# Cross attention in a two-layer decoder: token-major keys, one mixing group, query weights split one stage earlier, another order of the transposes

## The chip, the cores and the metric

The kernel runs on one core of a Trainium2 chip, in one launch. The metric is device time in microseconds (us) of one execution, as the median of some executions. The core has a matrix engine (TensorE, PE in the profile; its weight loads are PEld), VectorE (DVE), ScalarE (ACT), GpSimd (POOL) and the queue that starts transfers (SyncE, SP). Matmul results go to PSUM, eight banks of 128 x 512 float32; GpSimd works on SBUF alone.

## The reference

A decoder of two layers on 32 sequences of 64 tokens with 256 features, so 2048 rows. Each layer has three sublayers, `x = x + f(norm(x))`. The change touches two of the second layer: the state-space sublayer (only as the place where weights of the next one are prepared) and the cross attention behind it:

```python
q = rms(xn @ Wq + bq)  # 16 heads of 128; RMSNorm over each head, eps 1e-6
k = rms(ctx @ Wk + bk)  # 4 heads of 128
v = ctx @ Wv + bv
probs = softmax(q @ k.T / sqrt(128) + mask)  # each k/v head serves 4 query heads; 64 x 64 in each sequence
x = x + (probs @ v) @ Wo
```

`ctx` is the second input, 64 rows for each sequence. All of it is float32; the kernel's big products use pairs (below).

## The kernel before

The sublayers run one after another, with a barrier of all engines between them: `differential_attention`, `feature_attention`, `selected_update`, `state_space`, `grouped_attention` (the cross attention) and `mixture`.

The cross attention works in 16 tiles of 128 rows (two sequences each). One turn t of `pipeline` works at three tiles at once: it finishes tile t-1 (mixing and output product), does scores and softmax of tile t, and projects and norms the queries and keys of tile t+1; rows of tile t+2 are normed and transposed. Turns -2 to 0 fill the pipeline, turns 1 to 13 are a hardware loop, turns 14 to 16 drain it. Nothing is scheduled by a planner: each engine's order is the order of the code in its `turn`, and semaphores (`wait_ge`) hold an engine until another has got so far. So an instruction that waits holds all that stand behind it on its engine.

A precise float32 product is made as three passes (`three_passes`): the operands are split into a high part (float32r) and a low part (the rest), and high x high, low x high and high x low are added in PSUM. The high parts are copied by ScalarE or VectorE, the low parts are a subtraction on VectorE or GpSimd.

What a turn does, by name:
- `query(n, g)`: one of four quarters (512 columns) of the query projection, 6 matmuls of 512 columns, alternating between PSUM banks 0 and 1; VectorE adds the bias (`biased`, writes `q`), ScalarE squares (`square`, writes `q_scaled`), VectorE sums by head (`query_sums`, in two halves of 8 heads), ScalarE makes the inverse root by Ln and Exp (`query_rms`, writes `q_inv`), GpSimd multiplies (`scale_queries`, writes `q_scaled`), TensorE transposes (`turn_queries`, four quarters), ScalarE copies to `qT` (`take_queries`).
- Keys: `w_k` times `ctxT_k`, made feature-major in 16 matmul records of plain float32 of 128 columns (bank 2); ScalarE adds the bias and squares; the squares are split in two and summed over partitions by two matmuls with a matrix of ones (`k_sums`); ScalarE takes Ln and Exp of 128x512; VectorE multiplies to `kT`.
- Values: three passes of `ctxT_high`/`ctxT_low` with `w_v` (bank 3), which stand between the second and third quarter of `turn_queries`.
- Scores: `kT` and `qT` give scores with the keys on partitions, banks 4 and 5; ScalarE copies them (`scoresT`), TensorE transposes them to banks 6 and 7, VectorE adds the mask, takes the maximum, subtracts it; ScalarE takes Exp; VectorE sums, inverts (`inv`) and multiplies (`probs`). TensorE transposes `probs` to banks 4 and 5, ScalarE and VectorE make `probsT_high` and `probsT_low`.
- `mix(n, pair)`: values times probabilities, two of four key heads per pair; both pairs use banks 4 and 5, so the second waits until ScalarE (`take_mixed`) and VectorE (`mixed_low`) have read the first. Then the output product, 48 matmuls of 256 columns, into bank 6.

The query weights (2 MB) are loaded in the state-space stage to `staged`, and split at the start of the cross attention: VectorE and ScalarE copy the high halves, VectorE and GpSimd subtract.

## Time and profile before

| | us |
|---|---|
| median of 3 runs (1475.48 to 1477.69) | 1475.66 |
| the profiled execution's own time | 1476.98 |
| its span, first to last instruction | 1475.1 |

| engine | busy, share of the span |
|---|---|
| PE | 87% |
| DVE | 68% |
| ACT | 50% |
| POOL | 27% |

The cross attention runs from about 749 to 1170 us of the span, and its state-space predecessor from about 612 to 749 us. A turn in the middle of the cross attention takes 23.96 us. The share of the whole span says little on one stage; the stage is read from its own windows and from the timeline of one turn.

### The profile page before, as it was taken

The page shows a single profiled execution, that of the slowest core. Times are in us where ns is not written, and L with a number is a line of the kernel's source. Part 1 is how long each engine was busy: PE and PEld are TensorE (multiplying, and loading weights), DVE is VectorE, ACT ScalarE, POOL GpSimd, SP SyncE. Part 2 cuts the span into 40 slices and gives each one's busy share as a digit, 9 for nine tenths or more (in the row PEclk, how much of TensorE's full clock was granted, in tenths as well). Part 3 has the DMA queues.
Part 4 walks back from the last instruction along what each step waited for, and adds up shares of the span by engine and source line. Part 5 has one row for each costly group of instructions (what it writes and reads, how often), then busy time and mean ns, then how long its engine had stood idle before and what let it go on. Part 6 is the DMA issues. An engine that isn't in the chain of part 4 may idle for free. (4 is left out here: it accounts for less than half of the span.)

```text
span 1475.1 us, 28417 instructions
## 1 busy us (share of the span) xinstructions
PE 1290.2 (87%) x10124; PEld 1045.9 (71%) x10124; DVE 997.2 (68%) x1870; ACT 740.9 (50%) x1504; POOL 399.8 (27%) x488
## 2 busy tenths in 40 slices
PE   4888987199999984799958999999998599999998
PEld 3666665045555654478946878788887599999998
DVE  4767676267777745579855777777786557655555
ACT  1555555157777773430025667666666345333332
POOL 1112120344444410148625313132222021112210
PEclk9999999579999997579978999999999799999999
DMA  3000000345444400200030000000000110010001
GB/s 107 1 0 0 0 0 1 77 115 133 109 126 126 110 22 7 95 1 0 0 126 8 11 11 11 10 14 11 11 11 8 44 44 22 22 38 29 2 1 58
DMA packets 53385, 56.15 MB, mean 38 GB/s; under 512 B 7779, under 2 KB 49347, under 8 KB 50627
## 3 DMA queue, kind: packets, MB, share of 16 engines
q1 hardware_dynamic: 53318, 55.25, 13.5%
q8 instruction: 43, 0.70, 0.2%
q14 instruction: 24, 0.20, 0.0%
HBM read 44.35 MB, written 10.49 MB: 37 GB/s over the span
## 5 line engine op out<-in xcount | busy, mean ns | idle before, releaser
L677 DVE TENSOR_REDUCE fa_neg_max<-psum 128x2 f32<-128x512 f32 x256 | 167.7, 688 | 58.3 <-PE psum L854 57.6
L738 ACT ACTIVATE fa_probs<-psum 128x1024 f32<-128x1024 f32 x128 | 130.2, 1018 | 39.9 <-PE psum L865 36.2
L1607 PE MATMUL psum<-mo_xT_high,mo_w_high 128*128 128x256 f32 x512 | 145.6, 284 | 3.6 <-DVE mo_w_low L2278 3.6
L1607 PE MATMUL psum<-mo_xT_low,mo_w_high 128*128 128x256 f32 x512 | 145.2, 284 | 0.0
L1607 PE MATMUL psum<-mo_xT_high,mo_w_low 128*128 128x256 f32 x512 | 144.6, 282 | 0.0
L854 PE MATMUL psum<-fa_k_stack,fa_q_stack 72*128 72x256 bf16 x512 | 104.0, 288 | 35.6 <-DMA fa_k_stack<-k_parts 34.3
L2233 ACT ACTIVATE mo_silu<-psum 128x256 f32<-128x256 f32 x128 | 49.1, 384 | 159.9 <-PE psum L1607 159.8
L2367 DVE TENSOR_TENSOR mo_mid<-mo_silu,psum 128x256 f32<-128x256 f32 x128 | 53.7, 419 | 96.6 <-ACT mo_silu L2233 96.5
L1728 POOL TENSOR_TENSOR ga_q_scaled<-ga_q,ga_q_inv 128x1024 f32<-128x1024 f32 x32 | 62.1, 1941 | 165.9 <-ACT ga_q_inv L1769 165.9
L1607 PEld LDWEIGHTS psum<-mo_xT_high,mo_w_high 128*128 128x128 f32 x512 | 97.4, 190 | 4.0 <-DVE mo_w_low L2278 4.0
L1607 PEld LDWEIGHTS psum<-mo_xT_low,mo_w_high 128*128 128x128 f32 x512 | 97.5, 190 | 0.0
L1607 PEld LDWEIGHTS psum<-mo_xT_high,mo_w_low 128*128 128x128 f32 x512 | 97.4, 190 | 0.0
L854 PEld LDWEIGHTS psum<-fa_k_stack,fa_q_stack 72*128 72x128 bf16 x512 | 41.2, 100 | 77.2 <-DVE fa_neg_max L677 33.6
L865 PE MATMUL psum<-fa_q_stack,fa_k_stack 75*128 75x256 bf16 x512 | 79.2, 278 | 7.7 <-DMA fa_q_stack<-fa_max_rows 7.7
L258 POOL TENSOR_TENSOR da_keys<-da_rot,da_head_mask 128x1024 f32<-128x1024 f32 x16 | 30.4, 1897 | 186.7 <-DVE da_rot L386 186.7
L2179 POOL TENSOR_TENSOR mo_w_low<-mo_raw,mo_w_high 128x512 fp32r<-128x512 f32 x21 | 27.6, 1315 | 188.0 <-ACT mo_w_high L2208 188.0
L1607 PE MATMUL psum<-mo_w_high,mo_mid_high 128*128 128x256 f32 x256 | 72.3, 282 | 0.0
L1855 DVE TENSOR_TENSOR ga_q<-psum,ga_bias_q 128x512 f32<-128x512 f32 x64 | 42.7, 686 | 43.3 <-PE psum L1607 43.3
L1607 PE MATMUL psum<-mo_w_low,mo_mid_high 128*128 128x256 f32 x256 | 71.9, 281 | 0.0
L1607 PE MATMUL psum<-mo_w_high,mo_mid_low 128*128 128x256 f32 x256 | 71.7, 280 | 0.0
L879 PE MATMUL psum<-fa_probs,fa_values 128*32 128x256 f32 x1024 | 69.4, 389 | 1.1 <-ACT fa_probs L738 1.1
L2023 PE MATMUL psum<-ga_w_o_high,ga_mixedT_high 128*128 128x256 f32 x256 | 64.3, 294 | 0.0
(406 smaller groups left out, 3625.6 us busy)
## 6 DMA issues: line engine op xcount, KB each, us to landing
fa_q_stack<-q_parts SPq DMA_DIRECT2D x16, 576.0 KB
fa_k_stack<-k_parts SPq DMA_DIRECT2D x16, 576.0 KB
k_parts<-fa_parts SPq DMA_DIRECT2D x80, 64.0 KB, 2.6
q_parts<-fa_parts SPq DMA_DIRECT2D x48, 64.0 KB, 5.1
x<-in_x SPq DMA_DIRECT2D x4, 512.0 KB, 5.5
fa_context<-in_ctx SPq DMA_DIRECT2D x16, 128.0 KB, 2.1
staged<-in_ga_w_q SPq DMA_DIRECT2D x1, 2048.0 KB, 10.9
ga_ctxT_k<-in_ctxT SPq DMA_DIRECT2D x16, 128.0 KB, 2.2
```

Of the source, the lines that this page charges most:

```text
L258: nc.gpsimd.tensor_tensor(keys[:], rot[:, None, 2 * P:3 * P].to_broadcast([P, D_HEADS // 2, P]), head_mask[:, :, None].to_broadcast([P, D_ ...
L677: nc.vector.tensor_reduce(neg_max[:, b, :, h], ps[:, h % 2, :].rearrange("p (q k) -> p q k", q=2), AX.X, ALU.max, negate=True).then_inc(ma ...
L738: nc.scalar.activation(probs[:, g].rearrange("p h k q -> p h (k q)"), ps[:, 2 + 2 * (g % 2):4 + 2 * (g % 2), :], ACT.Exp).then_inc(exp_don ...
L854: done = nc.tensor.matmul(ps[:, h % 2, q * E:(q + 1) * E], q_stack[0:MAX_ROW, slot, b, h, q * P:(q + 1) * P], k_stack[0:MAX_ROW, slot, b, ...
L865: done = nc.tensor.matmul(ps[:, 2 + 2 * (g % 2) + h, k * E:(k + 1) * E], k_stack[0:STACK_ROWS, slot, b, 2 * g + h, k * P:(k + 1) * P], q_s ...
L879: done = nc.tensor.matmul(ps[32 * c:32 * c + 32, 6, half * E:(half + 1) * E], values[:, slot, k, 8 * b + h, :], probs[:, h // 2, h % 2, k, ...
L1607: done = nc.tensor.matmul(out, lhsT[i], rhs[j], start=start and k == 0, stop=stop and k == 2)
L1728: nc.gpsimd.tensor_tensor(q_scaled[:, columns].rearrange("p (h d) -> p h d", d=G_HD), q[:, columns].rearrange("p (h d) -> p h d", d=G_HD), ...
L1855: nc.vector.tensor_tensor(q[:, g * G_CHUNK:(g + 1) * G_CHUNK], ps[:, g % 2, :], bias_q[:, g * G_CHUNK:(g + 1) * G_CHUNK], ALU.add).then_in ...
L2023: nc.tensor.matmul(ps[:, 6, 0:E], mixedT_high[:, h], weight[:, h], start=(h == 0 and weight is w_o_high), stop=False)
L2233: nc.scalar.activation(silu[:, j % 4], ps[:, j % 4, 0:2 * P], ACT.Silu).then_inc(silu_ready, 1)
L2367: nc.vector.tensor_tensor(mid[:, j % 4], silu[:, j % 4], ps[:, j % 4, 2 * P:4 * P], ALU.mult).then_inc(mid_ready, 1)
```

## The change

- **Query weights.** `w_q_high` and `w_q_low` are now allocated with `staged` around both stages. They are filled in `state_space`: ScalarE copies (one piece of 1024 columns ahead of `keep_scores(0)`, three behind `decays(3)`), GpSimd subtracts in eight pieces of 512 columns (two ahead of its first `inputs`, six behind its last `own_rows`).
- **Keys token-major.** `key_or_value` computes keys as it does values: three passes, 6 matmuls of 512 columns, both from one `ctxT`. VectorE adds the bias (now a row of 512) and sums the squares over each head (128x512 to 128x4); ones, the split of the squares and their matmuls go; Ln and Exp work on 128x4. The raw keys are transposed (4 transposes), ScalarE writes `kT` with the gain as scale, and the keys' inverse root is applied as a scale by partition when the scores are copied to `scoresT` (4 operations of 128x256 for one of 128x1024).
- **Banks.** Scores go to banks 6 and 7. Mixing of the first pair goes to 6 and 7, of the second to 4 and 5, and both pairs run in one group, behind the first quarter of the query projection. The normed rows are transposed into bank 7.
- **Order on TensorE.** Before, in a turn: scores, query 0 and 1, score transposes, mix 0, query 2 and 3, mix 1, keys, output, transposes of `probs`, key sums, `turn_queries` 0 and 1, rows, values, `turn_queries` 2 and 3. Now: scores, query 0, mix 0 and 1, query 1 and 2, score transposes, query 3, keys, values, output, key transposes, rows, transposes of `probs`, `turn_queries` 0 to 3.
- **Order elsewhere.** On ScalarE the copy of `probsT_high` is now ahead of the second `query_rms`. VectorE takes the first two `mixed_low` ahead of query quarters 1 and 2 and of the mask. The loads at the stage's start are reordered, and one context tile is loaded once instead of twice.

TensorE, the end of a turn (`ident,ga_q_scaled` are the transposes of the queries, `ident,ga_probs` those of the probabilities, `w_v` the value projection), before:

```order
747 L2034 MATMUL psum<-ident,ga_probs 128x128 x8
748 L2040 MATMUL psum<-ga_k_high,ga_ones 128x512
749 L2041 MATMUL psum<-ga_k_low,ga_ones 128x512
...
754 L2050 MATMUL psum<-ident,ga_q_scaled 128x128 x4
755 L2057 REGISTER_ALU
756 L2061 MATMUL psum<-ident,ga_xn 128x128 x2
757 L1607 MATMUL psum<-ga_w_v_high,ga_ctxT_high 128x512
...
765 L2050 MATMUL psum<-ident,ga_q_scaled 128x128 x4
```

and now:

```order
767 L2056 MATMUL psum<-ga_w_o_high,ga_mixedT_low 128x256 x16
768 L2063 MATMUL psum<-ident,ga_k_raw 128x128 x4
769 L2066 REGISTER_ALU
770 L2068 MATMUL psum<-ident,ga_xn 128x128 x2
771 L2075 MATMUL psum<-ident,ga_probs 128x128 x8
...
776 L1993 MATMUL psum<-ident,ga_q_scaled 128x128 x4
777 L1991 REGISTER_ALU
778 L1993 MATMUL psum<-ident,ga_q_scaled 128x128 x8
```

The value projection, six matmuls that stood between the two halves of the query transposes, has left this place, and the key sums are gone.

ScalarE in the same part of a turn (`ga_q_log`, `ga_q_inv` are a half's `query_rms`, `ga_probsT_high` the copy of the transposed probabilities), before:

```order
455 L1810 CAST ga_k_high<-ga_k_squares 128x512
456 L1766 REGISTER_ALU
457 L1767 ACTIVATE ga_q_log<-ga_q_sum,ga_rms_eps 128x8
458 L1769 ACTIVATE ga_q_inv<-ga_q_log 128x8
459 L1813 ACTIVATE ga_k_log<-psum,ga_rms_eps 128x512
460 L1815 ACTIVATE ga_k_inv<-ga_k_log 128x512
461 L1818 CAST ga_probsT_high<-psum 128x1024
```

and now:

```order
457 L1840 ACTIVATE ga_kT<-psum,ga_gain 128x512
458 L1842 REGISTER_ALU
459 L1843 CAST ga_xT_high<-psum 128x256
460 L1846 CAST ga_probsT_high<-psum 128x1024
461 L1786 REGISTER_ALU
462 L1787 ACTIVATE ga_q_log<-ga_q_sum,ga_rms_eps 128x8
463 L1789 ACTIVATE ga_q_inv<-ga_q_log 128x8
```

The second half's inverse root, which stood ahead of the copy of the transposed probabilities, stands behind it.

The core of the diff:

```diff
+            pipeline(pool, turn, 2)
+            split_queries(2, Q_PIECES)
...
+            act.wait_ge(next_weights, 16)
+            query_highs(0, 1)
             keep_scores(0)
...
             def turn(t, valid):
                 if valid(t):
                     act.wait_ge(scored, t + 1)
-                    nc.scalar.copy(scoresT[:].rearrange("p (b c) -> p b c", b=2), ps[:, 4:6, :]).then_inc(scoresT_ready, 1)
+                    act.wait_ge(k_invs, t + 1)
+                    for j in range(G_KV):
+                        done = nc.scalar.activation(scoresT[:, j * E:(j + 1) * E], ps[:, 6 + j // 2, (j % 2) * E:(j % 2 + 1) * E], ACT.Copy,
+                                                    scale=k_inv[:, j:j + 1])
+                    done.then_inc(scoresT_ready, 1)
...
+                if valid(t):
+                    act.wait_ge(probsT_psum, t + 1)
+                    nc.scalar.copy(probsT_high[:].rearrange("p (b c) -> p b c", b=2), ps[:, 4:6, :]).then_inc(probsT_highs, 1)
+                if valid(t + 1):
                     query_rms(t + 1, 1)
+                    take_queries(t + 1, 0)
+                    take_queries(t + 1, 1)
...
+            def key_or_value(bank, high, low, psum_ready):
+                for c in range(KC):
+                    done = three_passes(nc, ps[:, bank, :], (ctxT_high[:, c], ctxT_low[:, c]), (high[:, c], low[:, c]),
+                                        start=(c == 0), stop=(c == KC - 1))
+                done.then_inc(psum_ready, 1)
...
                 if valid(t + 1):
                     pe.wait_ge(xT_ready, t + 2)
                     query(t + 1, 0)
+                if valid(t - 1):
+                    pe.wait_ge(v_lows, t)
+                    pe.wait_ge(probsT_lows, t)
+                    if valid(t):
+                        pe.wait_ge(scoresT_ready, t + 1)
+                    else:
+                        pe.wait_ge(x_ready, t)
+                    mix(t - 1, 0)
+                    mix(t - 1, 1)
+                if valid(t + 1):
                     query(t + 1, 1)
+                    query(t + 1, 2)
                 if valid(t):
                     pe.wait_ge(scoresT_ready, t + 1)
                     if started(t, 1):
-                        pe.wait_ge(x_ready, t)
+                        pe.wait_ge(mixed_lows, 4 * t - 2)
...
+                if valid(t + 1):
+                    turn_queries(t + 1, 0)
+                    turn_queries(t + 1, 1)
+                if valid(t + 1):
+                    turn_queries(t + 1, 2)
+                    turn_queries(t + 1, 3)
```

## Rows read from the trace of the kernel before

**Rows 1.** Windows: us, busy (count) of PE, PEld, DVE, ACT, POOL; clock, DMA.

```profile
784.00:1140.00 356.00, 340.92 (x2468) 285.32 (x2467) 266.99 (x392) 228.33 (x445) 100.63 (x68) 0.99 0.04 11
```

**Rows 2.** Timeline of PE, one turn: start, us, engine, line, operation [idle before].

```profile
899.93 0.50 PE L1607 MATMUL psum<-ga_w_q_high,ga_xT_high 128*128 128x512 f32 x1
...
902.79 1.04 PE L1995 MATMUL psum<-ident,ga_scoresT 128*128 128x128 f32 x8
...
908.01 0.39 PE L1969 MATMUL psum<-ga_probsT_high,ga_values_high 64*128 64x256 f32 x2 [0.32 <-DVE ga_mixedT_low L1868]
...
908.90 2.05 PE L2013 MATMUL psum<-ga_ctxT_k,ga_w_k 128*128 128x128 f32 x16
910.71 0.37 PE L2023 MATMUL psum<-ga_w_o_high,ga_mixedT_high 128*128 128x256 f32 x1
...
916.50 1.03 PE L2034 MATMUL psum<-ident,ga_probs 128*128 128x128 f32 x8
917.29 0.48 PE L2040 MATMUL psum<-ga_k_high,ga_ones 128*128 128x512 f32 x1
...
917.84 1.03 PE L2050 MATMUL psum<-ident,ga_q_scaled 128*128 128x128 f32 x8
...
920.90 1.09 PE L2050 MATMUL psum<-ident,ga_q_scaled 128*128 128x128 f32 x8 [0.23 <-ACT ga_qT L1822]
922.02 1.95 PE L1981 MATMUL psum<-ga_qT,ga_kT 128*64 128x256 f32 x16
923.89 0.50 PE L1607 MATMUL psum<-ga_w_q_high,ga_xT_high 128*128 128x512 f32 x1
```

**Rows 3.** Groups by form, 740 to 1170 us: line, operation, count, busy, mean ns, idle before.

```profile
L1728 POOL TENSOR_TENSOR ga_q_scaled<-ga_q,ga_q_inv 128x1024 f32<-128x1024 f32 x32 | 62.1, 1941 | 165.9 <-ACT ga_q_inv L1769 165.9
...
L1868 DVE SCALAR_TENSOR_TENSOR ga_mixedT_low<-psum,ga_bias_v,ga_mixedT_high 128x256 fp32r<-128x256 f32 x128 | 52.9, 476 | 10.3 <-ACT ga_mixedT_high L1773 10.3
...
L1855 DVE TENSOR_TENSOR ga_q<-psum,ga_bias_q 128x512 f32<-128x512 f32 x64 | 42.7, 686 | 43.3 <-PE psum L1607 43.3
L1773 ACT ACTIVATE ga_mixedT_high<-psum,ga_bias_v 128x512 fp32r<-128x512 f32 x64 | 40.2, 680 | 12.9 <-PE psum L1969 12.9
L1861 DVE TENSOR_REDUCE ga_q_sum<-ga_q_scaled 128x8 f32<-128x1024 f32 x32 | 38.7, 1209 | 0.0
...
L1818 ACT CAST ga_probsT_high<-psum 128x1024 fp32r<-128x1024 f32 x16 | 15.9, 997 | 5.9 <-PE psum L2034 5.9
...
L1720 POOL TENSOR_TENSOR ga_w_o_low<-staged,ga_w_o_high 128x512 fp32r<-128x512 f32 x8 | 10.5, 1338 | 0.0
```

**Rows 4.** Timeline of ACT and POOL in the turn of rows 2.

```profile
913.03 1.14 ACT L1805 ACTIVATE ga_k_raw<-psum,ga_bias_k 128x128 f32<-128x128 f32 x4
...
917.13 0.30 ACT L1767 ACTIVATE ga_q_log<-ga_q_sum,ga_rms_eps 128x8 f32<-128x8 f32 x1 [1.64 <-DVE ga_q_sum L1861]
...
917.75 1.90 POOL L1728 TENSOR_TENSOR ga_q_scaled<-ga_q,ga_q_inv 128x1024 f32<-128x1024 f32 x1 [0.63 <-ACT ga_q_inv L1769]
```

**Rows 5.** Timeline of DVE and POOL in turn 0, where they overlap.

```profile
792.94 2.18 DVE L1924 TENSOR_TENSOR ga_probs<-ga_probs,ga_inv 128x1024 f32<-128x1024 f32 x1
...
792.14 1.90 POOL L1728 TENSOR_TENSOR ga_q_scaled<-ga_q,ga_q_inv 128x1024 f32<-128x1024 f32 x1 [6.03 <-ACT ga_q_inv L1769]
```

**Rows 6.** Windows around waits of PE, columns as in rows 1.

```profile
120.00:150.00 30.00, 26.36 (x232) 19.68 (x231) 22.35 (x45) 16.14 (x35) 5.39 (x6) 1.00 0.00 0
1144.95:1148.30 3.35, 3.35 (x20) 3.13 (x21) 2.23 (x2) 2.21 (x3) 0.00 (x0) 0.50 0.00 0
1155.50:1158.50 3.00, 0.97 (x12) 0.77 (x12) 1.52 (x2) 1.00 (x2) 0.00 (x0) 1.00 0.02 5
1158.60:1161.00 2.40, 0.00 (x0) 0.00 (x0) 1.62 (x4) 0.75 (x2) 0.00 (x0) 0.50 0.00 0
```

**Rows 7.** Timeline of PE at the start of the cross attention.

```profile
756.64 0.69 PE L2061 MATMUL psum<-ident,ga_xn 128*128 128x128 f32 x2 [9.03 <-DVE ga_xn L113]
759.38 0.79 PE L1607 MATMUL psum<-ga_w_q_high,ga_xT_high 128*128 128x512 f32 x1 [2.05 <-DVE ga_w_q_low L1873]
```

More of the change, by code:

```diff
@@ L1357, in decays, with query_highs @@
                                          ACT.Exp).then_inc(decay_ready, 1)
+            def query_highs(first, last):
+                for k in range(first, last):
+                    columns = slice(2 * k * Q_PIECE, 2 * (k + 1) * Q_PIECE)
+                    nc.scalar.copy(w_q_high_flat[:, columns], staged[:, columns]).then_inc(w_q_highs, 1)
             keep_xT(0)
@@ L1756, in _ @@
             ln.on_scalar(act)
[L1757 to L1758 removed]
+            act.wait_ge(w_k_loaded, 16)
+            nc.scalar.copy(w_k_high[:], w_k).then_inc(w_k_highs, 1)
             def square(n, g):
```

351 lines of the change are left out of this document (160 added, 191 removed).

## The prediction

> **What bounds the kernel now.** I read first the windows of the cross-attention stage, then one of its turns on TensorE. From 784 to 1140 us TensorE is busy 340.92 of 356 us at a granted clock of 0.99 [rows 1]. In the timeline the turn from 899.93 to 923.89 takes 23.96 us, and the only brackets in it are 0.32 and 0.23 us [rows 2]: nearly every piece starts where the one before it leaves off. So a turn costs what TensorE has to do, and the softmax of VectorE and the norm of the queries are hidden behind it. Whatever the change does to TensorE's work is gained or lost one to one, as long as these stay hidden. That is the question here, since the change alters both.
>
> **TensorE's own work.** Keys: 910.71 - 908.90 = 1.81 us go; key sums: 917.84 - 917.29 = 0.55 go [rows 2]. In their place come six matmuls of 512 columns as in a quarter of the queries: two quarters take 902.79 - 899.93 = 2.86, so 1.43 at most and 1.37 in a run of them; and four transposes, at 0.79 for eight (917.29 - 916.50) some 0.45. Net -0.5. The wait before the second mixing (0.5 with its start-up) and the 0.3 before the third quarter of the query transposes go too. With no wait at all a turn would take 22.3 us, 1.6 less than now.
>
> **The chain that was hidden.** I walk it through one new turn, with zero where the scores end on TensorE. All operations but one are in the trace in the same or a like form.
> - ScalarE copies the scores in four parts with a scale. This form isn't in the trace. Four parts of 128x128 took 1.14 us [rows 4], which is the lower bound; four times the 0.60 or so of a 128x512 (0.68 by itself [rows 3]) is 2.4, the upper. At twice the size of the first and half that of the second I take 1.4, near the first. Then it copies the context (0.4), and squares query quarter 0, which VectorE has ready at 2.3: until 2.95. Then two `take_mixed`, 0.62 each back to back (0.68 alone [rows 3]), until 4.2. The mixing itself can't start before the scores are copied, at 1.5, only 0.1 later than TensorE is there.
> - VectorE now has no pause: from 4.25 on it does two `mixed_low` (each two operations of 0.41; 0.476 is their time alone [rows 3]), the biases of quarters 1 and 2, mask, values, maximum, subtraction, the keys' bias, quarter 3, two more `mixed_low`, sum, first query sum, reciprocal, multiplication. That is 3.3 for the `mixed_low`, 5 x 0.62 for operations of 128x512 (0.686 alone), 6 x 1.15 to 1.2 for those of 128x1024 (1.209 alone) [rows 3], and 0.3 for the reciprocal: 13.7 us, so `probs` is ready at 17.95.
> - TensorE has waited for it 0.4 us, transposes (0.8 and 0.2 until the result is there); ScalarE starts `probsT_high` at 19.1 and ends at 20.05 (0.997 alone [rows 3]). Only then comes the second `query_rms`, whose sums have been ready since 19.1. From its start to GpSimd's takes 917.75 - 917.13 = 0.62, and GpSimd 1.90 [rows 4]: 22.55.
> - TensorE has been done with the first half of the query transposes at 20.9. It waits 1.7 us here, having waited 0.9 for the first half (GpSimd's first product, 17.9 to 19.8). It then does 1.04 for the second half, and the scores, 923.89 - 922.02 = 1.87 [rows 2]: 25.5 us, and the next turn starts.
>
> So a turn is no longer 23.96 but about **25.5 us**, set by a ring: scores, first mixing, 13.7 us of VectorE, transposes of `probs`, their copy, `query_rms`, GpSimd, query transposes. Before, the value projection stood between the two halves of the transposes, and the second `query_rms` ran ahead of the copy; with both moved, what covered GpSimd's second product is gone. The second half waits for its product; the other late things in the turn (keys' root, `xT_low`, `probsT_low`) have 1 us or more. Between the scores of turn 1 and those of turn 15 lie 14 turns: 14 x 1.58 = +22.1 us. The walk applied in the same way to the turn before gives 24.0 for the measured 23.96, so I trust it to some 0.3 us a turn.
>
> **The port.** In turn 0 VectorE's product of `probs` (two SBUF inputs) began at 792.94 while GpSimd's `scale_queries` ran from 792.14 to 794.04, and it took 2.18 us, to 795.12, so until about one usual length after GpSimd's end [rows 5]. In the new turn VectorE's product (16.7 to 17.95) and GpSimd's first one (operands ready at 17.2) meet, VectorE being 0.4 us earlier: GpSimd then waits 0.7, which is in the walk and costs the ring nothing, as the second product decides.
> The Trainium skill (SBUF — State Buffer, "SBUF: two separate sides") states the rule behind it: whichever of GpSimd and a VectorE operation with two SBUF inputs starts first has the shared port pair for its whole instruction, and the other blocks. By that rule the sum stays as it is while VectorE is first; if GpSimd were first it would speak against this change, which is a rival below. Rows 5 agree with it: 2.18 us where the product alone takes about 1.2.
>
> **The clock.** A wait of 1.7 us after one of 0.9 and one of 0.4, with 1 us of work between each, is new. What follows such a stretch isn't settled by the trace of this stage. Near its end TensorE did 0.97 us of work in 3.00 and then the clock was at 0.50, that is 1.2 GHz, in the next window; and it stays there for a while: 1144.95 to 1148.30, 3.35 us of full work at 0.50 [rows 6], which costs 1.7 us. Against it stands a stretch of 30 us with 3.6 us of waits at a clock of 1.00 [rows 6]. The new turn has 3.0 us of waits within 5. It lies between the two, nearer to the first: I take a fall in every second turn, at 1.5 us of what it slows (some falls partly in a wait): 7 x 1.5 = +10.5. Bounds: 0 and 14 x 1.7 = 24.
>
> **Start, end, and the stage before.** The first query matmul starts at 759.38, after 9.03 and 2.05 us of waits for the row norm and the low part of the weights [rows 7]. Without the splitting there it follows the load and copy of `w_k` (done by about 755) and the first rows: about 755.9, -3.5. In the state-space stage, six GpSimd pieces of 1.34 us each [rows 3] come after its last work there, 8 us beside the last tiles; they may hold VectorE's sums (two SBUF inputs) by up to a piece each, twice. I take +1.5, from 0 to 3. ScalarE's copies lie in its gaps. In the drain the second mixing no longer waits for the first; other steps take longer: -1.
>
> **Sum.** +22.1 + 10.5 - 3.5 + 1.5 - 1 = +29.6, on the profiled execution's 1476.98: 1506.6. This execution is 1.3 above the median, so I say **1505**.
>
> **The rivals.**
> - *The clock doesn't fall*: the same ring, 1505 - 10.5 = 1494.5. For it: the waits are split by work. If it falls in all turns, 1505 + 13 = 1518.
> - *The ring is hidden, TensorE still bounds* (the other side): the turn is 22.3 us, -1.63 x 14 = -22.8, with -3 for the rest: 1475.7 - 26 = about 1450. It would need 3.2 us less in the ring, which the walk doesn't leave: VectorE's 13.7 us without a pause are measured durations. It decides when the second product ends before TensorE has done the first half, at 19.5 instead of 22.55.
> - *GpSimd gets the port first*: if VectorE's product starts after GpSimd's first one, it ends 1.2 us past 19.1 at 20.3, not 17.95. The ring grows by 2.4, x 14 = +33: about 1538. The margin is the 0.3 us reciprocal and a little.
> - *The ring is shorter than walked by half its excess*, e.g. by faster copies: 24.7 us, no fall of the clock, so 14 x 0.8 - 3 = +8: 1484; within that case it may also come out at no change, if the turn is 24.1.
>
> **How the numbers follow.** Forecast (ring, clock falling in about half of the turns, 1499 to 1512) 0.46; no fall 0.2; fall nearly always 0.1; port 0.05; shorter ring 0.1, of which no change 0.03; TensorE-bound 0.09. To hold 8 in 10 the range goes from 1486 (no fall, with the 0.3 us a turn and 3 us of the state-space stage) to 1521. Within 0.2% (3 us) a measurement can't tell it from no change. Faster by more 0.09, the same 0.03, slower 0.88.
>
> **What would show it.** In the profile after: a turn of 25.5 us; a bracket before the third quarter of the query transposes, released by GpSimd's `q_scaled`, of 1.7 us and one before the first of 0.9; VectorE without a pause from the first `mixed_low` to the product of `probs`; GpSimd's first product starting when VectorE's ends; clock below 1.00 in stretches of the stage; the first query matmul 3.5 us after where the stage's start puts the row norm, not 10. It is wrong if TensorE has no bracket there, or if the turn is below 24 us; the clock term is wrong alone if the stage's clock stays at 0.99 or above.

## The result, and the profile after

The changed kernel takes **1510.4 us** (median of 4 runs, 1505.6 to 1512.7) against 1475.6 us for the kernel before (median of 4 runs, 1474.8 to 1477.7): a ratio of **1.021**, 95% interval 1.017 to 1.026 (the two medians alone give 1.024). The profiled execution took 1509.0 us, its span 1507.2. The change makes the kernel about 2% slower; forecast were 1505 us and a range of 1486 to 1521.

Each turn can be measured from one of ScalarE's copies of the scores to the next. Before, the 14 steady turns take 23.88 us on average. After, ten of them take 25.57 and four 27.2 to 28.2 us.

The windows of the profile after (us; busy time and count of PE, PEld, DVE, ACT, POOL; granted clock; DMA) answer [rows 1]:

```profile
784.00:1140.00 356.00, 313.61 (x2165) 259.50 (x2164) 260.36 (x380) 189.06 (x392) 78.80 (x47) 0.98 0.02 5
```

TensorE is busy for 313.6 of 356 us; before it was 340.9. Outside four turns (below) it has not become slower, it waits. For what, the timeline of one new turn on PE shows, as [rows 2] did for the old one (start, duration, line, operation; in brackets the wait ahead and who ended it):

```profile
931.35 1.95 PE L2007 MATMUL psum<-ga_qT,ga_kT 128*64 128x256 f32 x16
933.23 0.50 PE L1627 MATMUL psum<-w_q_high,ga_xT_high 128*128 128x512 f32 x1
...
951.29 1.09 PE L2075 MATMUL psum<-ident,ga_probs 128*128 128x128 f32 x8 [0.20 <-DVE ga_probs L1932]
953.04 1.09 PE L1993 MATMUL psum<-ident,ga_q_scaled 128*128 128x128 f32 x8 [0.66 <-POOL ga_q_scaled L1748]
955.90 1.09 PE L1993 MATMUL psum<-ident,ga_q_scaled 128*128 128x128 f32 x8 [1.76 <-POOL ga_q_scaled L1748]
956.92 1.95 PE L2007 MATMUL psum<-ga_qT,ga_kT 128*64 128x256 f32 x16
958.79 0.50 PE L1627 MATMUL psum<-w_q_high,ga_xT_high 128*128 128x512 f32 x1
```

Three brackets stand near the end of the turn, and the longest, 1.76 us, is ahead of the second half of the query transposes. Before there was 0.23 us at this place, ended by ScalarE [rows 2]. Who is late is seen on the other engines in the same turn:

```profile
952.42 1.01 ACT L1846 CAST ga_probsT_high<-psum 128x1024 fp32r<-128x1024 f32 x1 [0.56 <-PE psum L2075]
953.32 0.30 ACT L1787 ACTIVATE ga_q_log<-ga_q_sum,ga_rms_eps 128x8 f32<-128x8 f32 x1
...
937.48 1.66 DVE L1884 SCALAR_TENSOR_TENSOR ga_mixedT_low<-psum,ga_bias_v,ga_mixedT_high 128x256 fp32r<-128x256 f32 x4 [1.85 <-ACT ga_mixedT_high L1793]
...
950.00 1.23 DVE L1932 TENSOR_TENSOR ga_probs<-ga_probs,ga_inv 128x1024 f32<-128x1024 f32 x1
951.14 1.21 DVE L1877 TENSOR_REDUCE ga_q_sum<-ga_q_scaled 128x8 f32<-128x1024 f32 x1
...
950.47 2.52 POOL L1748 TENSOR_TENSOR ga_q_scaled<-ga_q,ga_q_inv 128x1024 f32<-128x1024 f32 x1 [14.45 <-ACT ga_q_inv L1789]
953.94 1.90 POOL L1748 TENSOR_TENSOR ga_q_scaled<-ga_q,ga_q_inv 128x1024 f32<-128x1024 f32 x1 [0.96 <-ACT ga_q_inv L1789]
```

The query sums are there at about 952.3, but the logarithm starts only at 953.32, as the copy of the turned probabilities ends. GpSimd then multiplies until 955.84, and TensorE goes on at 955.90. Over the whole stage the waits of PE (total, times, longest) name the same pair:

```profile
PE psum L1993 <- POOL ga_q_scaled L1748: 41.3, 31, 3.1
PE psum L2075 <- DVE ga_probs L1932: 6.3, 15, 3.4
```

In the four longer turns the clock falls. This is one of them, on PE and in a window (columns as above):

```profile
1058.19 1.97 PE L1993 MATMUL psum<-ident,ga_q_scaled 128*128 128x128 f32 x8 [1.76 <-POOL ga_q_scaled L1748]
1060.09 3.68 PE L2007 MATMUL psum<-ga_qT,ga_kT 128*64 128x256 f32 x16
```

```profile
1060.00:1062.00 2.00, 2.00 (x11) 1.15 (x12) 0.00 (x0) 0.98 (x3) 0.00 (x0) 0.50 0.00 0
```

The transposes take 1.97 in place of 1.09 us and the scores 3.68 in place of 1.95, at half clock (1.2 GHz).

**Where the 32.1 us between the two spans are** (1507.2 - 1475.1). The landmarks are the last addition to `x` in the state-space stage, the first query matmul, and the first, second and last copy of the scores.

| stretch | before | after | difference |
|---|---|---|---|
| up to the last `x` of the state-space stage | 747.65 | 745.98 | -1.7 |
| to the first query matmul | 11.73 | 9.14 | -2.6 |
| to the first copy of the scores | 21.80 | 25.45 | +3.7 |
| first turn, between the first two copies | 23.19 | 24.90 | +1.7 |
| 14 turns: 14 x (25.57 - 23.88) | | | +23.7 |
| clock, in four of the 14 | | | +7.7 |
| to the end of the span | 336.4 | 336.0 | -0.4 |

The -1.7 isn't from the change: it is there, as -1.68, by 594 us, before any code that differs has run. In the profiles of the kernels below, the same landmark lies anywhere from 745.4 to 758.8 us with unchanged work ahead of it. A difference of some us between the totals of two kernels shows little by itself, so causes are read from the turns: ten of the changed kernel's 14 lie within 0.1 us of each other.

### The profile page after: what moved, and what is told of

It reads as the page before. It is cut to its first block and busy times, and to the rows that moved or that the text cites. A ratio compares the mean times of both kernels' runs of the same rounds, so it can differ in the third digit from the quotient of the medians.

```text
span 1507.2 us, 27997 instructions
## 1 busy us (share of the span) xinstructions
PE 1290.9 (86%) x9980; PEld 1041.6 (69%) x9996; DVE 1007.1 (67%) x1882; ACT 720.4 (48%) x1492; POOL 396.5 (26%) x482
## 5 line engine op out<-in xcount | busy, mean ns | idle before, releaser
L1748 POOL TENSOR_TENSOR ga_q_scaled<-ga_q,ga_q_inv 128x1024 f32<-128x1024 f32 x32 | 72.0, 2251 | 233.1 <-ACT ga_q_inv L1789 233.1
L1884 DVE SCALAR_TENSOR_TENSOR ga_mixedT_low<-psum,ga_bias_v,ga_mixedT_high 128x256 fp32r<-128x256 f32 x128 | 52.9, 476 | 38.3 <-ACT ga_mixedT_high L1793 38.3
L1993 PE MATMUL psum<-ident,ga_q_scaled 128*128 128x128 f32 x256 | 40.2, 307 | 41.3 <-POOL ga_q_scaled L1748 41.3
```

What stands on the lines that cost most here:

```text
L1748: nc.gpsimd.tensor_tensor(q_scaled[:, columns].rearrange("p (h d) -> p h d", d=G_HD), q[:, columns].rearrange("p (h d) -> p h d", d=G_HD), ...
L1884: done = nc.vector.scalar_tensor_tensor(low, mixed_of(j)[:, b], bias_v[:, j:j + 1], high.bitcast(F32), ALU.add, ALU.subtract)
L1993: done = nc.tensor.transpose(ps[:, g % 2, (h % 4) * P:(h % 4 + 1) * P], q_scaled[:, h * G_HD:(h + 1) * G_HD], ident[:])
```

## The experiments

**Theories.** *Ring*: a turn goes from the scores through the mixing, VectorE's string of work, the probabilities' transposes and their copy, the second `query_rms`, GpSimd's product and the query transposes back to the scores; only what shortens this ring counts. *Cover*: TensorE lacks the value projection between the two halves; whatever fills the wait is won. *Clock*: the rest comes from TensorE's clock falling behind its waits.

The runs together. The kernel before was run beside each group, with 1474.7 to 1477.2 us. A turn with the clock falling is counted if it is 0.7 us or more above the others of its kernel.

| kernel | us | ratio to before (95%) | turn at full clock | turns of 14 with a fall |
|---|---|---|---|---|
| changed | 1510.4 | 1.017 to 1.026 | 25.57 | 4 |
| e1 `query_rms` first | 1488.5 | 1.004 to 1.010 | 24.64 | 0 |
| e2 values between | 1510.1 | 1.013 to 1.027 | 25.57 | 6 |
| e3 waits filled | 1503.9 | 1.009 to 1.024 | 25.57 | 0 |
| e4 product in quarters | 1520.0 | 1.020 to 1.034 | 25.35 to 25.55 | 12 |
| e5 before, swapped | 1530.4 | 1.032 to 1.042 | 26.15, in one turn | 13 |
| e6 e1 and e2 | 1505.6 | 1.013 to 1.024 | 24.99 | 6 |
| e7 queries first | 1475.7 | 0.997 to 1.003 | 24.17 | 0 |
| e8 start | 1510.5 | 1.019 to 1.030 | 25.57 | 5 |
| e9 queries after the shift | 1450.7 | 0.979 to 0.987 | 22.42 | 0 |
| e10 port avoided | 1527.1 | 1.030 to 1.040 | not seen | 14 |
| e12 scores copied whole | 1512.6 | 1.019 to 1.029 | 25.38 | 8 |
| e13 e10, filled | 1512.8 | 1.016 to 1.029 | 25.70 | 0 |

### e1: the second query_rms first

```diff
-                if valid(t):
-                    act.wait_ge(probsT_psum, t + 1)
-                    nc.scalar.copy(probsT_high[:]...)
                 if valid(t + 1):
                     query_rms(t + 1, 1)
+                if valid(t):
+                    act.wait_ge(probsT_psum, t + 1)
+                    nc.scalar.copy(probsT_high[:]...)
                     take_queries(t + 1, 0)
```

> The changed kernel, with ScalarE's second pair of logarithm and exponential of the query norms issued ahead of its copy of the turned probabilities (before the change it stood there too). Ring theory: in the changed kernel GpSimd's second product of the queries starts only after the first one, which itself was started at 950.47, and the second pair of logarithm and exponential (953.3 to 953.96) waits behind the copy of 1.01 us; with it ahead, the second product starts about 0.8 us earlier, and every turn goes from 25.57 to 24.7 to 24.8 us: 14 turns give -11 to -12, so about 1498 us, or less where clock falls vanish with it. Rival (the missing cover alone: TensorE lacks 1.5 us of work between the halves, whatever ScalarE does): 25.57 stays, 1508 to 1511 us. Rival (the product itself can't start sooner since VectorE's product holds it): 25.57 stays too.

Measured: 14 turns of 24.63 to 24.69 us, none with a fall, and 1488.5 us, 22 us less than the changed kernel. The timeline of PE:

```profile
946.44 1.09 PE L2076 MATMUL psum<-ident,ga_probs 128*128 128x128 f32 x8 [0.20 <-DVE ga_probs L1933]
948.19 1.09 PE L1994 MATMUL psum<-ident,ga_q_scaled 128*128 128x128 f32 x8 [0.66 <-POOL ga_q_scaled L1748]
950.11 1.09 PE L1994 MATMUL psum<-ident,ga_q_scaled 128*128 128x128 f32 x8 [0.83 <-POOL ga_q_scaled L1748]
```

The wait ahead of the second half fell from 1.76 to 0.83, and the turn by exactly this 0.93 us. The turn came out as the ring theory had it, with a little more than the 0.8 us expected. The total fell by more: 14 x 0.93 = 13.0, the 7.7 us of the clock, and a first turn of 21.66 in place of 24.90. These make 24 us; the medians differ by 22. Two instructions of 0.5 us together, standing behind one of 1.0, were over half of the change's loss per turn (0.93 of 1.69).

### e2: the value projection back between the halves

```diff
-                    key_or_value(3, w_v_high, w_v_low, v_psum)
...
                     turn_queries(t + 1, 1)
+                    if started(t, 0):
+                        pe.wait_ge(v_lows, t + 1)
+                    key_or_value(3, w_v_high, w_v_low, v_psum)
...
                     turn_queries(t + 1, 2)
```

> The changed kernel, with the projection of the values (12 matrix products, 1.4 us on TensorE) put back from behind the keys to between the two halves of the query transposes, where it stood before the change. Cover theory (the wait of 1.76 us ahead of the second half is loss, since nothing covers it): turns of 25.57 - 1.4 = 24.2 us, about 1491 us. Ring theory (queries, biases, probabilities, their quotient, product on GpSimd, transposes: VectorE has no pause in it from TensorE's first query chunk on, so work that leaves TensorE ahead of the probabilities leaves a wait there and brings nothing): the wait ahead of the second half falls by 1.4 us, that ahead of the probabilities' transposes rises from 0.2 to 1.6 us, turns stay at 25.5 to 25.6, about 1510 us; fewer falls of the clock possible, at most -7.

```profile
957.75 1.09 PE L2072 MATMUL psum<-ident,ga_probs 128*128 128x128 f32 x8 [1.59 <-DVE ga_probs L1932]
959.50 1.52 PE L1993 MATMUL psum<-ident,ga_q_scaled 128*128 128x128 f32 x8 [0.66 <-POOL ga_q_scaled L1748]
...
963.38 1.06 PE L1993 MATMUL psum<-ident,ga_q_scaled 128*128 128x128 f32 x8
```

The bracket ahead of the second half is gone, and 1.39 us more stand ahead of the probabilities' transposes (1.59 in place of 0.20). The turn is 25.57 us, to the hundredth. The cover theory falls: work put into a wait is worth nothing if it is taken from ahead of another wait on the same ring. That the value projection left its place is not what the change costs in a turn at full clock.

### e3: the waits filled

```diff
+            def fill(n, count):
+                pe.wait_ge(kT_ready, n + 1)
+                for _ in range(count):
+                    nc.tensor.transpose(ps[:, 2, 0:P], ident[:], ident[:])
...
+                        fill(t + 1, 4)
                     turn_queries(t + 1, 0)
...
+                        fill(t + 1, 9)
                     turn_queries(t + 1, 2)
```

> The changed kernel, with 13 transposes of a constant into a free bank added in every turn of the steady loop, 4 just ahead of the first half of the query transposes (wait of 0.66 us) and 9 ahead of the second (wait of 1.76 us): 1.8 us more work of TensorE at the 0.136 us that one of its eight takes, none of it used. Both theories of the ring: turns stay at 25.57 us. Clock term: the four turns of 27.2 to 28.2 us (7.6 us above 25.57 together) go with the granted clock's falls to 0.50, since TensorE no longer stands still; about 1502 us. Rival (the falls have another cause, or TensorE's added work lies on the path): 1510 us or, with all 13 on the path, 1510 + 25.

Measured: all 14 turns 25.56 to 25.63, 1503.9 us, 6.5 less. The total alone would show little; that no turn has a fall fits the clock term. But four falls in one profile are few, and e1 had none with waits of 0.66 and 0.83; e10 and e13 below decide it.

### e4: the product in quarters

```diff
-                    scale_queries(0)
-                    scale_queries(1)
+                    for part in range(4):
+                        scale_queries(part)
...
-                pe.wait_ge(q_scaled_ready, 2 * n + (g // 2 + 1))
+                pe.wait_ge(q_scaled_ready, 4 * n + (g + 1))
```

> The changed kernel, with GpSimd's product of the queries in four instructions of four heads in place of two of eight (1.90 us each), and each TensorE group of four transposes waiting for its own quarter. Ring theory: the last product ends where it did or 0.1 to 0.2 us later (the fixed part of an instruction, twice), but the transposes of the third quarter run 0.9 us earlier and only four transposes and one copy of ScalarE lie behind the last: turns of 25.1 us (14 x -0.5 = -7, about 1503 us). Rival (the first half's transposes and what ScalarE copies behind them set the turn): 25.57 stays, 1510 us.

Measured: 1520.0 us, 9.6 more. The expectation missed twice. The two turns without a fall take 25.35 and 25.55, so the ring gained 0.2 us at best, not 0.5 (two quarters take 2.04 us together where a half took 1.90). And the clock fell in 12 turns of 14, with waits of 0.37, 1.24 and 0.37 us in place of 0.66 and 1.76.

### e5: the kernel before, with only this order changed

```diff
-                    query_rms(t + 1, 1)
                     act.wait_ge(k_sums, t + 2)
...
                     nc.scalar.copy(probsT_high[:]...)
+                if valid(t + 1):
+                    query_rms(t + 1, 1)
```

> The kernel BEFORE the change, with one thing done to it: ScalarE's second pair of logarithm and exponential of the query norms is issued behind its copy of the turned probabilities, as in the changed kernel. Theory from the run with the pair put first (24.64 in place of 25.57 us a turn): this order alone costs the kernel before as much or more, since there too the pair stands ahead of GpSimd's second product, and it must now also wait for the key scales (which stand ahead of that copy): turns of 23.85 + 1.0 to 1.9 = 24.9 to 25.8 us, 1490 to 1503 us, and clock falls on top. Rival (the pair's place costs only in the changed kernel, since there all of the queries' transposes follow at once): 23.85, 1476 us.

Measured: 1530.4 us, with turns of 27.26 to 27.38 (one of 26.15). On PE, ahead of the second half of the query transposes:

```profile
938.81 1.31 PE L2051 MATMUL psum<-ident,ga_q_scaled 128*128 128x128 f32 x8 [2.08 <-POOL ga_q_scaled L1728]
```

Against 0.23 us in [rows 2]. The same two instructions, moved the same way, cost the kernel before 53 us, although its value projection still stands between the halves. The one turn of 26.15 has no fall behind its wait of 2.09 us:

```profile
832.00:834.00 2.00, 2.00 (x20) 1.20 (x18) 0.42 (x1) 1.54 (x3) 0.00 (x0) 1.00 0.00 0
```

If it stands for the ring, the ring costs 2.3 us a turn, a little more than the 1.0 to 1.9 expected, and the clock 1.1; one turn is thin evidence for the split.

### e6: e1 and e2 together

> The changed kernel, with the pair of logarithm and exponential first and the values' projection between the two halves of the query transposes, so the two edits together. Alone they gave 24.64 and 25.57 us a turn. Ring theory: with the pair first, the second product ends 0.83 us after the first half's transposes, and a projection of 1.4 us between them is 0.6 us longer than that wait, while the projection taken from its old place leaves only a wait for the probabilities: 25.2 to 25.3 us a turn, 1497 to 1500 us. Cover theory (a wait that is filled is a gain): below 24.64, 1485 us or less.

Measured: 24.99 us a turn, 0.35 more than e1 alone, and six falls; 1505.6 us. The projection between the halves is not neutral but harmful once the product comes early. The expected 25.2 to 25.3 was 0.2 to 0.3 too high. The cover theory wanted a gain.

### e10 and e13: the port avoided, then the wait filled

In e10 the first half's query sums come before the last two `mixed_low`:

```diff
+                if valid(t + 1):
+                    query_sums(t + 1, 0)
                 if valid(t - 1):
                     mixed_low(t - 1, 2)
...
-                if valid(t + 1):
-                    query_sums(t + 1, 0)
```

> The changed kernel, with VectorE's first query sums ahead of its last two parts of the mixing's low half, so that GpSimd's first product ends before VectorE's product of the probabilities starts. The prediction held that the meeting at the port costs the turn nothing, since the second product decides: GpSimd's first product takes 1.90 in place of 2.52 us, TensorE's wait of 0.66 us ahead of the first half of the transposes goes, and the one ahead of the second half grows by as much; turns of 25.57, 1510 us (or up to 7 less, if fewer waits mean fewer clock falls). Rival (the first product's lateness is carried on to the second): 24.9 to 25.0 us, 1500 us.

```profile
929.87 1.09 PE L2075 MATMUL psum<-ident,ga_probs 128*128 128x128 f32 x8 [0.33 <-DVE ga_probs L1932]
930.80 1.04 PE L1993 MATMUL psum<-ident,ga_q_scaled 128*128 128x128 f32 x8
934.49 1.97 PE L1993 MATMUL psum<-ident,ga_q_scaled 128*128 128x128 f32 x8 [2.65 <-POOL ga_q_scaled L1748]
936.38 2.68 PE L2007 MATMUL psum<-ga_qT,ga_kT 128*64 128x256 f32 x16
```

```profile
934.50:936.40 1.90, 1.90 (x10) 1.57 (x10) 0.08 (x1) 0.59 (x1) 0.00 (x0) 0.50 0.00 0
```

Measured: 1527.1 us, 14 turns of 27.23 to 27.34. The brackets moved as expected, from 0.66 and 1.76 to none and 2.65, but the sentence on fewer falls was wrong: with the wait in one piece the clock falls in every turn. The window from 934.50 shows it at 0.50 directly behind the wait. The excess of those two rows is 0.88 + 0.73 = 1.6 us, and 27.3 - 1.6 is 25.7. To see whether this is all, e13 adds 17 transposes of a constant (as in e3) to this one wait.

> The kernel of port_avoided (changed kernel, first query sums earlier; turns of 27.23 to 27.34 us, TensorE waiting 2.65 us in one piece ahead of the second half of the query transposes, those at a granted clock of 0.50 behind it in every turn), with 17 transposes of a constant into a free bank in that wait, some 1.9 us of TensorE work that nothing uses. Clock theory (the ring is 25.57 us in port_avoided too, and the other 1.7 us of each turn are the second half's transposes, 1.97 in place of 1.09 us, and the scores, 2.7 in place of 1.9, at half clock): all turns 25.57 us, 14 x 1.73 = 24 us less, about 1503 us. Rival (the earlier query sums have lengthened the ring itself): 27.2 us a turn stay, 1527 us.

```profile
944.93 1.09 PE L1998 MATMUL psum<-ident,ga_q_scaled 128*128 128x128 f32 x8 [0.79 <-POOL ga_q_scaled L1748]
```

Measured: 14 turns of 25.69 to 25.77 us, no fall. So 1.6 us of each of e10's turns were the clock alone, and work that nobody uses takes them back. The ring itself is 0.13 longer than in the changed kernel, as VectorE's product comes 0.13 later (bracket 0.33 in place of 0.20). The total, 1512.8 us (1501.6 to 1517.1), lies 10 above the expectation: in its profile the last `x` of the state-space stage comes at 758.79 us, 13.0 later than in e10, with the same work ahead of it. Why it came later isn't shown.

### e12: the scores copied in one piece

Without the key scales, which this kernel leaves out of the result:

```diff
-                    for j in range(G_KV):
-                        done = nc.scalar.activation(scoresT[:, j * E:(j + 1) * E], ...,
-                                                    scale=k_inv[:, j:j + 1])
+                    done = nc.scalar.copy(scoresT[:]..., ps[:, 6:8, :])
```

> The changed kernel, with ScalarE's copy of the scores in one instruction without a scale, as the kernel before has it, in place of four with the key scales (the scale of the keys is left out of the result by this): 0.5 us less on ScalarE behind the scores. The prediction's walk starts with these 1.4 us (1.57 in the trace), but squares the first query chunk only when VectorE has it, at 2.3 us, 0.4 us behind the copy of the context; by that the copy is not on the ring: 25.57 us, 1510 us; TensorE's wait ahead of the mixing (0.16) goes. Rival (the copy in four is a part of the ring): 25.1 us, 1503 us.

Measured: turns of 25.38 us, so 0.19 less; the copy takes 1.01 in place of 1.57. Neither answer holds: a third of what the copy saves (0.56 us) comes off the ring. The way, as far as the traces show it, is in the changed kernel: the mixing waits 0.16 us for the copy, and behind it, by the transposes of the scores, VectorE's mask waits 0.18. In e12 both of these waits are gone:

```profile
935.06 0.39 PE L1977 MATMUL psum<-ga_probsT_high,ga_values_high 64*128 64x256 f32 x2 [0.16 <-ACT ga_scoresT L1807]
...
940.59 1.23 DVE L1908 TENSOR_TENSOR ga_probs<-psum,ga_mask 128x1024 f32<-128x1024 f32 x1 [0.18 <-PE psum L2030]
```

### e7 and e9: the changed kernel in another order

If the ring is the cause, the changed kernel's own instructions, reordered, should run at TensorE's 22.3 us. Nothing is added or left out. In e7 VectorE sums the first half's squares ahead of the row maxima and the second half's ahead of the probabilities' total (TensorE and ScalarE are reordered too; their order is given for e9, from which e7's differs in several places):

```
VectorE, changed: mask, values_low, top, shift, k_raw, bias 3, mixed_low 2 3, total, query_sums 0, reciprocal, product, query_sums 1
VectorE, e7:      mask, query_sums 0, top, shift, bias 3, k_raw, values_low, query_sums 1, mixed_low 2 3, total, reciprocal, product
VectorE, e9:      values_low, mask, top, shift, bias 3, query_sums 0, k_raw, query_sums 1, mixed_low 2 3, total, reciprocal, xT_low, product
TensorE, e9:      scores, query 0, mix 0 1, query 1 2, turn scores, query 3, keys, turn x, out_high 0 1 2, values, out_high 3,
                  out_low 0 1, turn queries 0, turn keys, turn queries 1, out_low 2 3, turn queries 2 3, turn probabilities
ScalarE, e9:      scores, take_mixed 0 to 3, square 0, values_high, square 1, context, square 2 3, xT_high, query_rms 0,
                  exponential, query_rms 1, take_queries 0, key squares, take_queries 1, kT, key root, take_queries 2 3, probsT_high
```

> The changed kernel's instructions, all of them, in another order inside the turn: VectorE sums the squares of the first half of the queries ahead of the row maxima and those of the second half ahead of the probabilities' totals, ScalarE takes each pair of logarithm and exponential directly behind, so that GpSimd's two products run beside the softmax and not behind it; TensorE transposes the queries between the parts of the output projection and turns the probabilities last, and the projections of keys and values lie between the output projection's parts. Ring theory (the turn is long because VectorE does softmax and query norms one behind the other and GpSimd's 3.8 us stand behind both): the ring falls under TensorE's own 22.3 us, which then sets the turn: 22.4 to 23.0 us, no clock falls, 1456 to 1466 us, below the kernel before. Rival (another ring, by the turned probabilities' two copies and the mixing behind them): 23.9 or more, 1476 us or more.

Measured: 24.17 us a turn and 1475.7 us (10 runs; the interval holds 1): level with the kernel before, 35 us below the changed one, but not the 22.4 to 23.0 expected. DVE and POOL show a part of the reason:

```profile
930.45 2.48 DVE L1933 TENSOR_TENSOR ga_probs<-ga_probs,ga_top 128x1024 f32<-128x1024 f32 x1
...
929.95 1.90 POOL L1748 TENSOR_TENSOR ga_q_scaled<-ga_q,ga_q_inv 128x1024 f32<-128x1024 f32 x1 [2.61 <-ACT ga_q_inv L1789]
```

GpSimd had begun 0.50 us ahead of VectorE's subtraction, which takes 1.22 us elsewhere; now it takes 2.48 and ends 1.1 us after GpSimd. This is the rival "GpSimd gets the port first", in another place of the turn. By the rule of the Trainium skill (SBUF — State Buffer, "SBUF: two separate sides") the one that starts first, GpSimd or a VectorE instruction with two SBUF inputs, has the shared ports for its whole instruction. The traces agree, and both directions are now in them: 2.52 for GpSimd's 1.90 in the changed kernel and 2.48 for VectorE's 1.22 here. In e9 no product meets such an instruction.

How much of the turn the meeting cost was not isolated. TensorE waits 0.82 us a turn for GpSimd's second product in e7, and e9's turn is 1.75 shorter; the rest lies in short pauses between the pieces, and e9 orders the pieces on TensorE and ScalarE differently as well:

```profile
938.46 0.66 PE L2015 MATMUL psum<-ident,ga_q_scaled 128*128 128x128 f32 x4 [0.82 <-POOL ga_q_scaled L1748]
```

> The changed kernel's instructions in a third order, after the run of queries_first, whose turns were 24.17 and not 22.6 us: there VectorE's subtraction of the row maxima took 2.48 us in place of 1.23, since GpSimd's first product had begun 0.47 us ahead of it. Here the first query sums stand behind that subtraction and the bias of the fourth query chunk, so that GpSimd starts on the first product only when the subtraction is done, and ends the second one before VectorE begins its own product; ScalarE takes all four parts of the mixing ahead of the squares, and TensorE has the keys' projection between the last query chunk and the output projection. Port theory (the 1.25 us of that wait, and what it pushed back, is all that kept the turn above TensorE's own 22.3 us): no VectorE instruction of 128x1024 above 1.3 us in a steady turn, turns of 22.5 to 23.1 us, 1452 to 1462 us, below both kernels. Rival (another ring holds it, such as scores, mixing, its copies, the output projection): 23.6 to 24.2 us, 1468 to 1476 us.

The window, the waits of PE from 790 to 1110 us, and the timeline of DVE and POOL:

```profile
784.00:1100.00 316.00, 308.92 (x2230) 263.94 (x2229) 260.20 (x388) 194.80 (x407) 71.50 (x49) 0.99 0.02 6
```

```profile
PE psum L1999 <- ACT ga_scoresT L1807: 2.3, 14, 0.2
```

```profile
921.56 1.23 DVE L1934 TENSOR_TENSOR ga_probs<-ga_probs,ga_top 128x1024 f32<-128x1024 f32 x1
...
929.41 1.21 DVE L1959 TENSOR_TENSOR ga_probs<-ga_probs,ga_inv 128x1024 f32<-128x1024 f32 x1
...
925.17 3.75 POOL L1748 TENSOR_TENSOR ga_q_scaled<-ga_q,ga_q_inv 128x1024 f32<-128x1024 f32 x2 [5.64 <-ACT ga_q_inv L1789]
```

Measured: **1450.7 us** (6 runs, 1448.2 to 1452.6), ratio to the kernel before 0.983 (0.979 to 0.987), turns of 22.4 us. Both products lie between subtraction and product, all at their own length. TensorE's one wait in a steady turn is 0.16 us. It beats both kernels: the change's instructions are the cheaper ones, its order gave that away.

### e8: the start alone

The loads of the key and value weights go behind the mask's, the key weights' copy behind the first `xT_high`, and the rounding of the output weights one turn later:

```diff
-            sp.dma_start(w_k, chunked(dram["ga_w_k"])).then_inc(w_k_loaded, 16)
-            sp.dma_start(w_v, chunked(dram["ga_w_v"])).then_inc(w_v_loaded, 16)
...
             sp.dma_start(mask[:], mask_rows).then_inc(loaded, 16)
+            sp.dma_start(w_k, chunked(dram["ga_w_k"])).then_inc(w_k_loaded, 16)
+            sp.dma_start(w_v, chunked(dram["ga_w_v"])).then_inc(w_v_loaded, 16)
...
-            act.wait_ge(w_k_loaded, 16)
-            nc.scalar.copy(w_k_high[:], w_k).then_inc(w_k_highs, 1)
...
+                if isinstance(t, int) and t == -2:
+                    act.wait_ge(w_k_loaded, 16)
+                    nc.scalar.copy(w_k_high[:], w_k).then_inc(w_k_highs, 1)
...
+                if isinstance(t, int) and t == 0:
+                    dve.wait_ge(w_o_loaded, 16)
...
-                if isinstance(t, int) and t == -1:
-                    dve.wait_ge(w_o_loaded, 16)
```

> The changed kernel, edited ahead of its steady turns alone: the loads of the key and value weights are issued behind the small ones (so that the mask, for which VectorE and ScalarE wait 4.88 and 5.58 us, lands sooner), the key weights' copy stands behind that of the first turned tokens, and the rounding of the output weights on VectorE (2.3 us, in conflict with GpSimd's first products, which took 5.79 in place of 3.80) stands one turn later, in VectorE's pause. Expected: the first scores 3 to 4 us earlier against the end of the stage before, the steady turns as they were (25.57 and some with a fallen clock): 1506 to 1508 us. Rival (the start is bound by the key weights' halves, which come later by the edit): no gain, 1510 us.

Measured: from the end of the state-space stage to the first copy of the scores 32.86 us in place of 34.59, so -1.7, half of what was expected; the first turn then took 25.57 in place of 24.90. The products take 3.88 in place of 5.79 us, but the keys' matmuls now wait 3.89 us for weights, where the changed kernel has no such wait:

```profile
764.14 0.76 PE L1627 MATMUL psum<-ga_w_k_high,ga_ctxT_high 128*128 128x512 f32 x1 [3.89 <-POOL ga_w_v_low L1761]
```

The rival holds in part. In the total (1510.5 us) nothing is left of it.

## Why the prediction was right, point by point

Its time was 5.4 us below the measured one (0.4%), inside the forecast's own 1499 to 1512.

**TensorE's own work**: 22.3 us without a wait was said; e9 has 22.42, with one wait of 0.16. The number is right, its derivation isn't complete: the terms listed (0.5, 0.5 and 0.3) take 1.3 from 23.96, which gives 22.7, and not the 1.6 claimed.

**The ring**: 25.5 was said, 25.57 measured. Step by step, with zero at the end of the scores (933.23 in the turn above): first `mixed_low` 4.25 said, 4.25 measured; probabilities ready 17.95 and 18.0; `probsT_high` from 19.1 and 19.2; second product until 22.55 and 22.6; waits 0.4, 0.9, 1.7 and 0.20, 0.66, 1.76. The copy in four, taken as 1.4 from bounds of 1.14 and 2.4, takes 1.57. Off were two small things: VectorE has one pause, of 0.18 us at the mask, and the copy that causes it was held to be off the ring (e12: 0.19 us). The mean of the turns before is 23.88, not the 23.96 of the turn in [rows 2]; so the term measured +23.7 where +22.1 was said.

**What covered the product**: the prediction named two moves, the value projection and the second `query_rms`, as if they counted alike. They don't. e1 gives 0.93 us a turn for the order on ScalarE, e2 nothing for the projection.

**The port**: said was that GpSimd waits 0.7 us and it costs the ring nothing. It waits 0.62 (2.52 - 1.90), and e13, where the meeting is gone, has no shorter turn. Right for the ring. Not foreseen: without it the wait is one piece, and the clock falls in every turn.

**The clock**: +10.5 from seven falls of 1.5 us was said; in the profile it is +7.7 from four, of 1.6 to 1.7 us each and once 2.6, and the stage's granted clock is 0.98 where 0.99 or more would have spoken against the term. The size of a fall was right, the number a choice between 0 and 14. The variants show how close both ends were, with 0 of 14 in e3 and 14 of 14 in e10.

**The start**: this term failed. Said was -3.5, up to the first query matmul, and nothing behind it. The matmul did come 2.6 us earlier. But the first copy of the scores came 1.1 later by the same landmark, and the first turn took 1.7 more: +2.8 in all, 6.3 off.

```profile
755.12 0.80 PE L1627 MATMUL psum<-w_q_high,ga_xT_high 128*128 128x512 f32 x1 [3.92 <-DVE ga_xT_low L1940]
...
771.07 1.94 PE L1993 MATMUL psum<-ident,ga_q_scaled 128*128 128x128 f32 x8 [3.09 <-POOL ga_q_scaled L1748]
774.97 1.94 PE L1993 MATMUL psum<-ident,ga_q_scaled 128*128 128x128 f32 x8 [1.96 <-POOL ga_q_scaled L1748]
776.84 3.68 PE L2007 MATMUL psum<-ga_qT,ga_kT 128*64 128x256 f32 x16
...
765.96 0.69 DVE L1918 TENSOR_TENSOR ga_k_raw<-psum,ga_bias_k 128x512 f32<-128x512 f32 x1 [2.35 <-PE psum L1627]
...
767.16 2.33 DVE L1877 TENSOR_REDUCE ga_q_sum<-ga_q_scaled 128x8 f32<-128x1024 f32 x2
770.75 2.32 DVE L1946 CAST ga_w_o_high<-staged 128x4096 fp32r<-128x4096 f32 x1
...
769.03 5.79 POOL L1748 TENSOR_TENSOR ga_q_scaled<-ga_q,ga_q_inv 128x1024 f32<-128x1024 f32 x2 [4.85 <-ACT ga_q_inv L1789]
```

In the changed kernel VectorE sums the queries behind the keys' bias, so the early queries wait for the keys' projection (765.96); GpSimd's two products meet the rounding of the output weights and take 5.79 us in place of 3.80; and TensorE stands still for 3.09 and 1.96 us and does the first scores at half clock. The prediction moved the first instruction of a stage and took it for the stage. Two other numbers point the same way: with the query sums earlier, in e7 and e9, the first copy of the scores comes 28.96 and 27.80 us behind the last `x`, in place of 34.59; and with e1's order on ScalarE the first turn takes 21.66 us in place of 24.90.

**The state-space stage**: +1.5 was said, with 0 as lower bound; in these two profiles it is 0.0 (153.3 us from the same transposes just ahead of the stage to its last `x`, from 594.36 to 747.65 before, and from 592.68 to 745.98 after). One piece of the weights did hold VectorE, 1.92 us in place of 0.96, and it was covered: the wait behind it is 0.74 us, where the kernel before has 1.71. From its first VectorE instruction to the last `x` the stage takes 135.7 us in both, but 134.0 to 142.7 in the eleven other kernels with the same code there, so one profile doesn't settle a term of 1.5.

```profile
735.86 1.92 DVE L1500 TENSOR_TENSOR ss_sums<-ss_outputs 128x768 f32<-128x768 f32 x1
738.52 0.42 DVE L1506 TENSOR_TENSOR x<-x,psum 128x256 f32<-128x256 f32 x1 [0.74 <-PE psum L1597]
```

**The drain**: -1 said, -0.4 measured.

So ring and clock together were forecast at +32.6 and measured at +31.4. The start was 6.3 us too low, the ring 1.6 and the drain 0.6; state-space stage and clock were 4.3 too high, and the unchanged work ahead gave -1.7. That makes 2.5 of the 5.4; the other 2.9 lie between the profiled executions and the medians. The closeness of the total is partly luck; that of the turn is not.

**Still open**: why the clock falls in four turns of the changed kernel and not in the other ten. Ahead of a fall the waits are the same 0.20, 0.66 and 1.76 us. The falls are in the tenth and the last three of the 14 turns here; in e8, whose steady turns have the same instructions, they are in the second to the sixth. No run here tells the turns apart.

## What to carry to other kernels

Walk the ring of waits instruction by instruction, with back-to-back durations from the trace, and ask of each move whether it shortens the ring or only shifts a wait along it: here two tiny activations behind a copy cost 0.93 us a turn, and a projection of 1.4 us, put back into the wait, brought none. When an engine waits, put everything that feeds the slowest helper ahead of what is needed later, then look at whether the helper's instructions meet VectorE's with two SBUF inputs, and which comes first: in the order of e9 the same instructions run 4% faster than in the changed kernel. Price a start up to the first result of the stage, not up to its first instruction.

## What the runs showed of the hardware that I had not expected

How the waits of a turn are split changes how often the clock falls, though no rule comes out of it. Waits of 0.33 and 2.65 us gave falls in 14 turns of 14 (e10), 0.20, 0.66 and 1.76 in 4 and 5 of 14 (changed kernel, e8), nearly the same, 0.20, 0.66 and 1.77, in 8 (e12), 0.20, 0.66 and 0.83 in none (e1); but 0.37, 1.24 and 0.37, which are shorter in sum than the changed kernel's, gave 12 of 14 (e4). A fall costs 0.8 to 1.7 us, once 2.6, and transposes of a constant in the wait take it back (e13: 1.6 us a turn), although nobody uses them.

GpSimd's wait at the port, 0.62 us, cost the ring nothing (e13). VectorE's, 1.26 us in e7, lies on the way to GpSimd's second product, for which TensorE waits 0.82 us a turn. In both cases the first engine was half a microsecond ahead, VectorE in one and GpSimd in the other. The VectorE instructions differ too, so that the order of the two made the whole difference isn't shown.
